# Second norm and residual of the attention stage taken two token tiles late instead of one

## The chip, the cores and the metric

The kernel runs on the 8 cores of one Trainium2 chip. All cores run the same program, each on its own 2048 tokens; they exchange nothing. The time is the device time of the slowest core in microseconds (us). Engines are named as the profile does: PE is TensorE, DVE is VectorE, ACT is ScalarE, POOL is GpSimd, SP is the engine that only issues DMAs.

## What is computed

The input x is 16384 tokens of 1024 numbers (f32). LN stands for the plain layer norm without weights.

```python
# attention over the 16 heads of ONE token (not over the sequence)
qkv = (LN(x) @ W_qkv + b_qkv).reshape(B, S, 16, 192)       # q, k, v of 64 each
scores = einsum('bshd,bsgd->bshg', q, k) / 8
context = einsum('bshg,bsgd->bshd', softmax(scores), v)
x = x + LN(context @ W_out + b_out)
# 8 dense experts, summed
h = LN(x)
acc = sum over e of (silu(h @ Wg[e]) * (h @ Wu[e])) @ Wd[e]
x = x + LN(acc)
```

## The kernel before

One program has three stages: attention (to about 1464 us), experts (64 groups of 512 hidden columns, matmuls almost without a gap, to about 6830 us) and a last norm. The change is in the attention stage alone.

**Tiling.** The 2048 tokens are 16 tiles of 128, one token per partition. Tile t passes through seven steps, S1 to S7, each a Python function that appends instructions to one list per engine. Every engine runs its own list strictly in the order in which it was written; the engines meet only at semaphores. The order in which the loop calls S1 to S7 is therefore the whole schedule.

- S1(t), DVE with ACT: layer norm of x. `ln_stats` (L142 to L160) is three passes over 1024 columns on DVE (L144, L145, L147), a few one-column operations, then Ln and Exp on ACT (L155, L157) and a last DVE operation (L159). DVE then writes `ln1` (L231).
- S2(t), PE with ACT: eight transposes of `ln1` (L207); ACT copies them out to `ln1T` (L210). All three transposing steps (S2, S5, S7) share L207 and L210 and the two halves of `ps_tr`.
- S3(t), PE with ACT: six groups of one bias matmul (L256) and eight matmuls (L260), which alternate between the two halves of `ps_mm`; ACT copies each group out to `qkv` (L265). The third group needs the first one copied out, and so on.
- S4(t), DVE: a copy of v (`vtc`, L275), scores, softmax (its Exp is on ACT, L308), and the weighted sum into `ctxt` (L340). It begins with a wait for the last copy of S3(t).
- S5(t), PE with ACT: eight transposes of `ctxt`, a copy to `ctxT` (L210), then two groups of one bias matmul (L361) and eight matmuls (L364) into `ps_att`, which has two halves, by the parity of t. It waits until S6(t-2) has read the same half (`tok_lna`).
- S6(t), DVE with ACT: `ln_stats_psum` on `ps_att`: a sum on DVE (L164), a Square on ACT (L166) into `scr`, a sum of that on DVE (L168), one-column operations, Ln and Exp on ACT (L176, L178), then DVE normalizes (L380) and adds to x (L384).
- S7(t), DVE with ACT and PE: `ln_stats` on the new x, `ln2tok` (L396), eight transposes and a copy to `ln2T` (L210), which the experts read. After every fourth tile, SP stores the group of four tiles of x (L404) and then, for the first two groups, loads a new group into the same buffer (L407).

The loop of before calls, in iteration t: S2(t), S1(t+1), S3(t), S5(t-1), S6(t-1), S7(t-1), S4(t). In ACT's list this makes, in this order: copy of S2(t); Ln and Exp of S1(t+1); six copies of S3(t); copy of S5(t-1); Square, Ln, Exp of S6(t-1); Ln, Exp and copy of S7(t-1); Exp of S4(t).

The expert stage loads its first weights only when all of the attention stage is over: POOL waits for the last counts of PE, DVE and ACT.

Of the kernel before, what the change touches and what calls it, by code (L numbers as in the profile page):

```python
# [27 lines left out]
def build(mode='full', nt_lim=NT):  # L28
# [46 lines left out]
    def op(k, fn, ch=None, n=1):  # L75
        if ch is not None:
            ch.v += n
            em(k, lambda e, fn=fn, h=ch.h, n=n: fn(e).then_inc(h, n))
            return ch.v
        em(k, fn)  # L80
        return None
# [60 lines left out]
    def ln_stats(src_fn, par):  # L142
        st_ = stats[:, par]
        op('v', lambda v: v.tensor_mul(scr[:, par], src_fn(), src_fn()))  # L144
        op('v', lambda v: v.reduce_sum(st_[:, 0:1], src_fn(), axis=AX.X), VV)  # L145
        VV.wt('v')
        op('v', lambda v: v.reduce_sum(st_[:, 1:2], scr[:, par], axis=AX.X))  # L147
        op('v', lambda v: v.tensor_scalar_mul(st_[:, 0:1], st_[:, 0:1], 1.0 / D), VV)
        VV.wt('v')
        op('v', lambda v: v.tensor_scalar_mul(st_[:, 1:2], st_[:, 1:2], 1.0 / D))  # L150
        op('v', lambda v: v.tensor_mul(st_[:, 2:3], st_[:, 0:1], st_[:, 0:1]), VV)
        VV.wt('v')
        op('v', lambda v: v.tensor_sub(st_[:, 2:3], st_[:, 1:2], st_[:, 2:3]), VV)
        VV.wt('s')
        op('s', lambda s: s.activation(st_[:, 3:4], st_[:, 2:3], AF.Ln, bias=consts[:, 0:1], scale=1.0), SS)  # L155
        SS.wt('s')
        op('s', lambda s: s.activation(st_[:, 4:5], st_[:, 3:4], AF.Exp, scale=consts[:, 1:2]), SS)  # L157
        SS.wt('v')
        return op('v', lambda v: v.tensor_scalar(st_[:, 5:6], st_[:, 0:1], st_[:, 4:5], -1.0,  # L159
                                                 ALU.mult, ALU.mult), VV)  # L160

    def ln_stats_psum(src_fn, par):
        st_ = stats[:, par]
        op('v', lambda v: v.reduce_sum(st_[:, 0:1], src_fn(), axis=AX.X), VV)  # L164
        VV.wt('s')
        op('s', lambda s: s.activation(scr[:, par], src_fn(), AF.Square), SS)  # L166
        SS.wt('v')
        op('v', lambda v: v.reduce_sum(st_[:, 1:2], scr[:, par], axis=AX.X))  # L168
        op('v', lambda v: v.tensor_scalar_mul(st_[:, 0:1], st_[:, 0:1], 1.0 / D), VV)
        VV.wt('v')  # L170
        op('v', lambda v: v.tensor_scalar_mul(st_[:, 1:2], st_[:, 1:2], 1.0 / D))
        op('v', lambda v: v.tensor_mul(st_[:, 2:3], st_[:, 0:1], st_[:, 0:1]), VV)
        VV.wt('v')
        op('v', lambda v: v.tensor_sub(st_[:, 2:3], st_[:, 1:2], st_[:, 2:3]), VV)
        VV.wt('s')
        op('s', lambda s: s.activation(st_[:, 3:4], st_[:, 2:3], AF.Ln, bias=consts[:, 0:1], scale=1.0), SS)  # L176
        SS.wt('s')
        op('s', lambda s: s.activation(st_[:, 4:5], st_[:, 3:4], AF.Exp, scale=consts[:, 1:2]), SS)  # L178
        SS.wt('v')
        return op('v', lambda v: v.tensor_scalar(st_[:, 5:6], st_[:, 0:1], st_[:, 4:5], -1.0,  # L180
                                                 ALU.mult, ALU.mult), VV)
# [18 lines left out]
    def transpose_batch(src_fn, dst):  # L200
        c = n_trb[0]; n_trb[0] += 1
        s_ = c % 2
        if c - 2 in tok_tr_evac:
            QE.wt('t', tok_tr_evac[c - 2])
        tr_tok = None
        for k in range(8):
            tr_tok = op('t', lambda t, k=k, s_=s_: t.transpose(ps_tr[:, s_, k], src_fn(k), ident[:]),  # L207
                        TB if k == 7 else None)
        TB.wt('s', tr_tok)
        ev = op('s', lambda s, s_=s_, dst=dst: s.activation(dst, ps_tr[:, s_], AF.Copy), QE)  # L210
        tok_tr_evac[c] = ev
        return tr_tok, ev
# [4 lines left out]
    def S1(t_i):  # L217
        j, i = divmod(t_i, 4)
        jp = j % 2
        p2 = t_i % 2  # L220
        xt = xf[:, jp, i]
        if t_i == 0:
            GI.wt('v'); VV.wt('v')
        if i == 0:
            XJ = XLa if j % 2 == 0 else XLb
            XJ.wt('v', 16 * (j // 2 + 1))
        ln_stats(lambda xt=xt: xt, p2)
        VV.wt('v')
        if t_i >= 2:
            TB.wt('v', tok_ln1_tr[t_i - 2])  # L230
        tok_ln1_w[t_i] = op('v', lambda v, xt=xt, p2=p2: v.tensor_scalar(  # L231
            ln1[:, p2], xt, stats[:, p2, 4:5], stats[:, p2, 5:6], ALU.mult, ALU.add), VE)

    def S2(t_i):
        p2 = t_i % 2
        VE.wt('t', tok_ln1_w[t_i])
        if t_i == 0:
            GI.wt('t')
        if t_i >= 2:
            MM.wt('v', tok_qkv_mm[t_i - 2])  # L240
        trt, ev1 = transpose_batch(lambda k, p2=p2: ln1[:, p2, k * 128:(k + 1) * 128], ln1T[:, p2])
        tok_ln1_tr[t_i] = trt
        tok_ln1T_ev[t_i] = ev1
# [103 lines left out]
    def S5(t_i):  # L347
        p2 = t_i % 2
        VV.wt('t', tok_hm_done[t_i])
        if t_i >= 2:  # L350
            MM.wt('v', tok_wout_mm[t_i - 2])
        trt2, ev2 = transpose_batch(lambda k, p2=p2: ctxt[:, p2, k * 128:(k + 1) * 128], ctxT[:, p2])
        tok_ctx_tr[t_i] = trt2
        QE.wt('t', ev2)
        if t_i == 0:
            WIo.wt('t')
        if t_i >= 2:
            LNA.wt('t', tok_lna[t_i - 2])
        mt = None
        for n in range(2):  # L360
            op('t', lambda t, n=n, p2=p2: t.matmul(ps_att[:, p2, n], ones1[:],  # L361
                                                   bo_sb[:, n * 512:(n + 1) * 512], start=True, stop=False))
            for k in range(8):
                mt = op('t', lambda t, n=n, k=k, p2=p2: t.matmul(  # L364
                    ps_att[:, p2, n], ctxT[:, p2, k], wout_sb[:, k, n * 512:(n + 1) * 512],
                    start=False, stop=(k == 7)), MM if k == 7 else None)
        tok_wout_mm[t_i] = mt

    def S6(t_i):
        j, i = divmod(t_i, 4)  # L370
        jp = j % 2
        p2 = t_i % 2
        xt = xf[:, jp, i]
        mt = tok_wout_mm[t_i]
        MM.wt('v', mt)
        MM.wt('s', mt)
        psa = lambda p2=p2: ps_att[:, p2].rearrange("p a b -> p (a b)")
        ln_stats_psum(psa, p2)
        VV.wt('v')
        op('v', lambda v, p2=p2, psa=psa: v.tensor_scalar(  # L380
            tmpl[:], psa(), stats[:, p2, 4:5], stats[:, p2, 5:6], ALU.mult, ALU.add), LNA)
        tok_lna[t_i] = LNA.v
        LNA.wt('v', tok_lna[t_i])
        op('v', lambda v, xt=xt: v.tensor_add(xt, xt, tmpl[:]), VV)  # L384
        VV.wt('v')

    def S7(t_i):
        j, i = divmod(t_i, 4)
        jp = j % 2
        p2 = t_i % 2  # L390
        xt = xf[:, jp, i]
        ln_stats(lambda xt=xt: xt, p2)
        VV.wt('v')
        if t_i >= 2:
            QE.wt('v', tok_ln2_ev[t_i - 2])
        w_ln2 = op('v', lambda v, xt=xt, p2=p2: v.tensor_scalar(  # L396
            ln2tok[:, p2], xt, stats[:, p2, 4:5], stats[:, p2, 5:6], ALU.mult, ALU.add), VE)
        VE.wt('t', w_ln2)
        _, ev = transpose_batch(lambda k, p2=p2: ln2tok[:, p2, k * 128:(k + 1) * 128],
                                ln2T[:, :, t_i * 128:(t_i + 1) * 128])  # L400
        tok_ln2_ev[t_i] = ev
        if i == 3:
            QE.wt('y', ev)
            op('y', lambda e, jp=jp, j=j: e.dma_start(xsp_r[:, j], xf[:, jp]), SP, 16)  # L404
            if j + 2 < NJ:
                SP.wt('y')
                op('y', lambda e, j=j, jp=jp: e.dma_start(xf[:, jp], x_r[:, j + 2]),  # L407
                   XLa if (j + 2) % 2 == 0 else XLb, 16)

    S1(0)  # L410
    for t_i in range(nt_lim):
        S2(t_i)
        if t_i + 1 < nt_lim:
            S1(t_i + 1)
        S3(t_i)
        if t_i >= 1:
            S5(t_i - 1)
            S6(t_i - 1)
            S7(t_i - 1)
        S4(t_i)  # L420
    S5(nt_lim - 1)
    S6(nt_lim - 1)
    S7(nt_lim - 1)

# [277 lines left out]
```

How the kernel before makes its waits and increments, by code:

```python
        def wt(self, k, tok=None):  # L71
            t_ = self.v if tok is None else tok
            em(k, lambda e, h=self.h, t=t_: e.wait_ge(h, t))
# [1 line left out]
    def op(k, fn, ch=None, n=1):  # L75
        if ch is not None:
            ch.v += n
            em(k, lambda e, fn=fn, h=ch.h, n=n: fn(e).then_inc(h, n))
            return ch.v
        em(k, fn)
        return None
```

## Time and profile before

| | us |
|---|---|
| runs shown of before | 6951.82 and 7245.42, median 7098.62 |
| the profiled execution | 6951.28 |
| its span, first to last instruction, slowest core | 6949.7 |
| spans of the eight cores | 6936.9 to 6949.7 |
| mean granted TensorE clock (1.0 is 2.4 GHz) | 0.911 on seven cores, 0.912 on one |

The profile records each instruction with its start, its duration and, where its engine had been idle, for how long and which engine's semaphore ended the idle time ("[17.27 <-PE ps_att L364]"). Busy time of an engine that waits for nothing is not what limits a stage; the chain of waits has to be followed from one engine to the next. PE's matmuls overlap, so that eight matmuls in a row show one common duration.

### The profile page before, as it was taken

Reading aid. Unit: us, or ns where it says so; the run is one execution under the profiler, and the core shown is the slowest. Engines: PE = TensorE matmul, PEld = TensorE weight load, DVE = VectorE, ACT = ScalarE, POOL = GpSimd, SP = SyncE. Lnnn points to the kernel's source line nnn. Section 1 sums busy time; section 2 is a strip of 40 time slices with the busy share of each in tenths; the row PEclk is TensorE's granted clock in tenths of the full one; section 3 lists DMA queues with packets and bytes.
Section 4 is the critical chain, followed back from the end, with each engine's and each line's share of the span. In section 5 each row is a group of like instructions: output and inputs, shape, how many; then the busy total and the mean of one; then the engine's idle time right before and its main releaser. Section 6 shows DMA issues by size and latency. Waiting matters only on the chain.

```text
span 6949.7 us, 71337 instructions; the slowest of 8 cores (6936.9 to 6949.7 us)
## 1 busy us (share of the span) xinstructions
PE 5718.3 (82%) x26240; PEld 2567.3 (37%) x26240; DVE 3208.7 (46%) x4436; ACT 792.4 (11%) x1347; POOL 164.9 (2%) x202
## 2 busy tenths in 40 slices
PE   2222222249999999999999999999999999999992
PEld 0111011114444444444444444444444444444441
DVE  4666666743434434334343343443433434334347
ACT  0111111101111111111111111111111111111111
POOL 0000000000000000000000000000000000000000
PEclk7666666669999999999999999999999999999996
DMA  3000000022222222222222222222222222222212
GB/s 73 0 24 0 24 0 12 0 49 37 37 37 37 38 46 45 37 37 37 37 37 37 37 37 43 47 39 37 37 37 37 37 37 37 39 47 43 37 19 97
DMA packets 173421, 247.85 MB, mean 36 GB/s; under 512 B 3616, under 2 KB 134688, under 8 KB 171552
## 3 DMA queue, kind: packets, MB, share of 16 engines
q0 software_dynamic: 169056, 209.74, 18.4%
q1 hardware_dynamic: 4032, 33.56, 1.3%
q8 instruction: 223, 3.65, 0.2%
q14 instruction: 110, 0.90, 0.0%
HBM read 436.22 MB, written 16.78 MB: 65 GB/s over the span
## 4 chain that ended last, share of the span: by engine, by line
PE 80%; DVE 14%; issue 3%; ACT 1%; DMA 1%; another core or an unknown queue 0%; DVEq 0%; ACTq 0%; POOL 0%; POOLq 0%
PE ps_g L508 25%; PE ps_u L513 25%; PE ps_d L539 25%; DVE prod L332 2%; DVE prod L290 2%; PE ps_mm L260 2%; DVE prod L328 2%; DVE prod L286 2%; PE ps_att L364 1%; DVE stats L147 1%; DVE scr L144 1%; DVE stats L145 1%; DMA wd_b<-wd 0%; PE ps_mm L256 0%
## 5 line engine op out<-in xcount | busy, mean ns | idle before, releaser
L523 DVE TENSOR_TENSOR hbuf<-silb,ps_u 128x512 bf16<-128x512 bf16 x1024 | 703.7, 687 | 2888.9 <-PE ps_u L513 2888.9
L508 PE MATMUL ps_g<-ln2T,wg_b 128*128 128x512 bf16 x8192 | 1936.9, 379 | 34.5 <-DMA wd_b<-wd 34.5
L513 PE MATMUL ps_u<-ln2T,wu_b 128*128 128x512 bf16 x8192 | 1936.4, 379 | 0.0
L539 PE MATMUL ps_d<-hbuf,wd_b 128*128 128x512 bf16 x8192 | 1809.7, 379 | 0.0
L549 DVE TENSOR_TENSOR acc<-ps_d,acc 128x512 f32<-128x512 f32 x2016 | 1393.0, 692 | 331.1 <-PE ps_d L539 303.7
L508 PEld LDWEIGHTS ps_g<-ln2T,wg_b 128*128 128x128 bf16 x8192 | 802.0, 98 | 1001.9 <-issue 36.4
L513 PEld LDWEIGHTS ps_u<-ln2T,wu_b 128*128 128x128 bf16 x8192 | 801.8, 98 | 967.9 <-issue 2.2
L539 PEld LDWEIGHTS ps_d<-hbuf,wd_b 128*128 128x128 bf16 x8192 | 801.6, 98 | 966.5
L519 ACT ACTIVATE silb<-ps_g 128x512 bf16<-128x512 f32 x1024 | 612.3, 598 | 4675.3 <-PE ps_g L508 4675.3
L256 PE MATMUL ps_mm<-bq_sb,ones 1*128 1x512 bf16 x96 | 49.0, 510 | 723.0 <-ACT ln1T L210 371.0
L256 PEld LDWEIGHTS ps_mm<-bq_sb,ones 1*128 1x128 bf16 x96 | 9.2, 96 | 773.1 <-issue 773.1
L260 PE MATMUL ps_mm<-wqkv_sb,ln1T 128*128 128x512 bf16 x768 | 245.2, 477 | 0.0
L207 PE MATMUL ps_tr<-ident,ln2tok 128*128 128x128 bf16 x128 | 16.2, 307 | 242.3 <-DVE ln2tok L396 242.3
L480 POOL DMA_DIRECT2D wg_b<-wg x64 | 57.0, 890 | 6491.5 <-PE ps_d L539 5030.1
L332 DVE TENSOR_TENSOR prod<-prod 128x2048 bf16<-128x2048 bf16 (+2 forms) x192 | 162.4, 846 | 20.0
L290 DVE TENSOR_TENSOR prod<-prod 128x2048 bf16<-128x2048 bf16 (+2 forms) x192 | 149.9, 781 | 20.7 <-DVE prod L290 1.0
L328 DVE TENSOR_TENSOR prod<-probsn,vtc 128x4096 bf16<-128x4096 bf16 x64 | 146.3, 2285 | 3.7 <-DVE probsn L314 3.7
L286 DVE TENSOR_TENSOR prod<-qkv 128x4096 bf16<-128x4096 bf16 x64 | 146.0, 2281 | 0.0
L164 DVE TENSOR_REDUCE stats<-ps_att 128x1 f32<-128x1024 f32 x16 | 19.6, 1224 | 259.6 <-PE ps_att L364 259.6
L260 PEld LDWEIGHTS ps_mm<-wqkv_sb,ln1T 128*128 128x128 bf16 x768 | 80.4, 115 | 139.8 <-issue 100.6
L207 PEld LDWEIGHTS ps_tr<-ident,ln2tok 128*128 128x128 bf16 x128 | 12.4, 138 | 249.7 <-issue 249.7
L616 PE MATMUL ps_c<-ident,acc_bf 128*128 128x128 bf16 x128 | 14.8, 290 | 101.0 <-DVE acctok L620 99.9
(80 smaller groups left out, 976.4 us busy)
## 6 DMA issues: line engine op xcount, KB each, us to landing
wg_b<-wg POOLq DMA_DIRECT2D x64, 1024.0 KB, 9.5
wu_b<-wu POOLq DMA_DIRECT2D x64, 1024.0 KB, 13.7
wd_b<-wd POOLq DMA_DIRECT2D x64, 1024.0 KB, 17.8
xf<-x SPq DMA_DIRECT2D x4, 2048.0 KB, 10.6
xspill<-xf SPq DMA_DIRECT2D x4, 2048.0 KB, 7.0
xrel<-xspill SPq DMA_DIRECT2D x4, 2048.0 KB, 8.1
out<-outb SPq DMA_DIRECT2D x16, 512.0 KB, 2.6
wqkv_sb<-wqkv POOLq DMA_DIRECT2D x1, 6144.0 KB, 52.5
```

Source lines behind the costliest of these rows:

```text
L144: op('v', lambda v: v.tensor_mul(scr[:, par], src_fn(), src_fn()))
L260: mt = op('t', lambda t, n=n, b=b, k=k, p2=p2: t.matmul(ps_mm[:, b], ln1T[:, p2, k], wqkv_sb[:, k, n * 512:(n + 1) * 512], start=False, st ...
L286: op('v', lambda v, sl=sl, qap=qap, kap=kap: v.tensor_tensor(prod[:, sl].rearrange("p (h g d) -> p h g d", h=4, g=16), qap, kap, ALU.mult) ...
L290: op('v', lambda v, sl=sl, half=half: v.tensor_add(bass.AP(prod, sl * 4096, [[8192, 128], [1024, 4], [64, 16], [1, half]]), bass.AP(prod, ...
L328: op('v', lambda v, sl=sl, pap=pap, vap=vap: v.tensor_tensor(prod[:, sl].rearrange("p (h d g) -> p h d g", h=4, d=64), pap, vap, ALU.mult) ...
L332: op('v', lambda v, sl=sl, half=half: v.tensor_add(bass.AP(prod, sl * 4096, [[8192, 128], [1024, 4], [16, 64], [1, half]]), bass.AP(prod, ...
L508: gt = op('t', lambda t, par=par, kh=kh, kd=kd, bk=bk, toks=toks: t.matmul(ps_g[:, bk], wg_b[:, par, kd, kh * 128:(kh + 1) * 128], ln2T[:, ...
L513: ut = op('t', lambda t, par=par, kh=kh, kd=kd, bk=bk, toks=toks: t.matmul(ps_u[:, bk], wu_b[:, par, kd, kh * 128:(kh + 1) * 128], ln2T[:, ...
L519: silu_tok[c] = op('s', lambda s, bk=bk, c=c: s.activation(silb[:, c % 2], ps_g[:, bk], AF.Silu), SIL)
L523: mul_tok[c] = op('v', lambda v, kh=kh, bk=bk, c=c, q=q: v.tensor_tensor(hbuf[:, q % 2, kh], silb[:, c % 2], ps_u[:, bk], ALU.mult), MUL)
L539: dt_ = op('t', lambda t, par=par, m=m, mi=mi, kh=kh, q=q: t.matmul(ps_d[:, mi], wd_b[:, par, kh, m * 128:(m + 1) * 128], hbuf[:, q % 2, k ...
L549: tok = op('v', lambda v, m=m, mi=mi, toks=toks: v.tensor_add(acc[:, m, toks], ps_d[:, mi], acc[:, m, toks]), ACC)
```

## The change

S6 and S7 are called for tile t-2 instead of t-1 in iteration t, from iteration 2 on. S5 stays at t-1. Behind the loop, S6(14) and S7(14) follow S5(15), and then come S6(15) and S7(15). No instruction is added or removed; all sizes and buffers stay.

```diff
         S3(t_i)
         if t_i >= 1:
             S5(t_i - 1)
-            S6(t_i - 1)
-            S7(t_i - 1)
+        if t_i >= 2:
+            S6(t_i - 2)
+            S7(t_i - 2)
         S4(t_i)
     S5(nt_lim - 1)
+    if nt_lim >= 2:
+        S6(nt_lim - 2)
+        S7(nt_lim - 2)
     S6(nt_lim - 1)
     S7(nt_lim - 1)
```

## Rows read from the trace of the kernel before

**Rows 1.** Head of the profile's page.
```profile
span 6949.7 us, 71337 instructions; the slowest of 8 cores (6936.9 to 6949.7 us)
```

**Rows 2.** Stretches: length, busy us (instructions) by engine, granted clock, DMA share, GB/s.
```profile
134.00:1464.00 1330.00, 366.75 (x1428) 139.73 (x1427) 919.53 (x1110) 141.16 (x253) 0.00 (x0) 0.62 0.02 8
...
2000.00:4000.00 2000.00, 2000.00 (x9269) 906.70 (x9267) 799.23 (x1159) 230.82 (x386) 60.46 (x72) 1.00 0.23 39
```

**Rows 3.** Waits of 0 to 1400 us: total, times, longest.
```profile
DVE stats L164 <- PE ps_att L364: 249.9, 15, 17.5
...
ACT scr L166 <- DVE stats L164: 93.5, 15, 8.7
```

**Rows 4.** Timeline of iteration 8: start, duration, engine, line, operation [idle before].
```profile
723.32 2.05 PE L260 MATMUL ps_mm<-wqkv_sb,ln1T 128*128 128x512 bf16 x8
...
747.33 1.06 ACT L265 ACTIVATE qkv<-ps_mm 128x512 bf16<-128x512 f32 x2
...
760.27 1.02 ACT L210 ACTIVATE ctxT<-ps_tr 128x1024 bf16<-128x1024 bf16 x1
...
763.99 1.90 PE L364 MATMUL ps_att<-wout_sb,ctxT 128*128 128x512 bf16 x8
766.00 1.23 DVE L164 TENSOR_REDUCE stats<-ps_att 128x1 f32<-128x1024 f32 x1 [17.27 <-PE ps_att L364]
767.32 1.02 ACT L166 ACTIVATE scr<-ps_att 128x1024 f32<-128x1024 f32 x1 [6.03 <-DVE stats L164]
768.44 1.22 DVE L168 TENSOR_REDUCE stats<-scr 128x1 f32<-128x1024 f32 x1 [1.22 <-ACT scr L166]
...
779.89 0.81 DVE L396 TENSOR_SCALAR ln2tok<-xf,stats 128x1024 bf16<-128x1024 f32 x1 [0.18 <-DVE stats L159]
...
782.06 1.02 ACT L210 ACTIVATE ln2T<-ps_tr 128x1024 bf16<-128x1024 bf16 x1 [2.67 <-PE ps_tr L207]
...
854.70 1.22 DVE L164 TENSOR_REDUCE stats<-ps_att 128x1 f32<-128x1024 f32 x1 [17.38 <-PE ps_att L364]
```

**Rows 5.** Timeline of iteration 15, the last, which has no S1.
```profile
1373.61 1.22 DVE L164 TENSOR_REDUCE stats<-ps_att 128x1 f32<-128x1024 f32 x1 [9.80 <-PE ps_att L364]
1374.92 1.02 ACT L166 ACTIVATE scr<-ps_att 128x1024 f32<-128x1024 f32 x1 [8.73 <-DVE stats L164]
```

**Rows 6.** Timeline of iterations 0 (first row) and 1.
```profile
72.15 1.02 DVE L275 COPY vtc<-qkv 128x1024 bf16<-128x1024 bf16 x1 [43.89 <-ACT qkv L265]
...
139.40 0.60 ACT L265 ACTIVATE qkv<-ps_mm 128x512 bf16<-128x512 f32 x1 [1.55 <-PE ps_mm L260]
...
145.62 1.23 DVE L164 TENSOR_REDUCE stats<-ps_att 128x1 f32<-128x1024 f32 x1 [16.44 <-PE ps_att L364]
146.94 1.02 ACT L166 ACTIVATE scr<-ps_att 128x1024 f32<-128x1024 f32 x1 [6.03 <-DVE stats L164]
...
160.17 1.02 DVE L275 COPY vtc<-qkv 128x1024 bf16<-128x1024 bf16 x1
```

**Rows 7.** Timeline behind the loop: S5(15), S6(15), S7(15).
```profile
1440.29 1.02 ACT L210 ACTIVATE ctxT<-ps_tr 128x1024 bf16<-128x1024 bf16 x1 [26.16 <-PE ps_tr L207]
...
1448.70 1.23 DVE L164 TENSOR_REDUCE stats<-ps_att 128x1 f32<-128x1024 f32 x1 [9.77 <-PE ps_att L364]
...
1451.43 1.22 DVE L168 TENSOR_REDUCE stats<-scr 128x1 f32<-128x1024 f32 x1 [1.51 <-ACT scr L166]
...
1462.88 0.81 DVE L396 TENSOR_SCALAR ln2tok<-xf,stats 128x1024 bf16<-128x1024 f32 x1 [0.18 <-DVE stats L159]
```

**Rows 8.** Timeline, PE alone: third and fourth S3 group of iteration 1, fourth of iteration 14.
```profile
129.01 3.60 PE L260 MATMUL ps_mm<-wqkv_sb,ln1T 128*128 128x512 bf16 x8
...
133.08 1.92 PE L260 MATMUL ps_mm<-wqkv_sb,ln1T 128*128 128x512 bf16 x8
...
1285.06 2.77 PE L260 MATMUL ps_mm<-wqkv_sb,ln1T 128*128 128x512 bf16 x8
```

**Rows 9.** DMA issues of 0 to 1600 us: count, KB each, median us to landing.
```profile
xf<-x SPq DMA_DIRECT2D x4, 2048.0 KB, 10.6
```

## The prediction

> **What bounds the kernel now.** I read the page's head first [rows 1], then the stretches [rows 2]. They show two different kernels. From 134 to 1464 us, DVE is busy 919.5 of 1330 us (69%) and PE 366.8 (28%); from 2000 to 4000 us PE is busy all the time, at a granted clock of 1.00. The change only touches the first, so its whole effect must come from what DVE waits for there. The table of waits gives the price of the thing that the change is about [rows 3]: DVE sat idle 249.9 us, 15 times, in front of the first operation of S6 (L164) until the S5 matmuls were done, and once more 9.77 us behind the loop [rows 7], 259.7 us in all. The same table has a second row that matters more: ACT sat idle 93.5 us before the Square of S6 (L166).
>
> The timeline of iteration 8 [rows 4] shows why these differ. DVE is free at 766.00 - 17.27 = 748.73. But ACT starts the first two S3 copies only at 747.33, right behind Ln and Exp of S1(9), and the third and later groups of S3 can't run before that. So the stretch from 748.7 to 766.0 is, in this order: four S3 groups on PE with their copies on ACT, the ctxT copy (760.27 to 761.29), 18 matmuls of S5 (to 765.9), then L164. DVE, ACT and PE form one chain; DVE's next work is S6 and behind it S4.
>
> **What the change does, iteration 2 to 14.** L164 of tile t-2 reads matmuls that were done in the iteration before, so it starts at about 748.73 and is over 1.3 us later. The Square that follows is on ACT, and ACT's list still has the S3 copies and the ctxT copy ahead of it, for S5(t-1) is still called before S6(t-2). It can start at 761.29 and not at 767.32. L168 waits for it, and all else on DVE is behind L168. So what goes is ACT's idle time before the Square: 6.03 us here, made of the S5 matmuls and of L164. The stall of 17.27 is not removed: about 11 us of it stay and stand before L168 instead of L164. For 13 iterations: 93.5 less iteration 1 (6.03, [rows 6]) less iteration 15 (8.73, [rows 5]) = **78.7 us gained**, 6.06 each.
>
> These rows carry the choice between 6 and 17 us. The second S3 group was done at 725.4 (723.32 + 2.05, [rows 4]), the first before it, and ACT had nothing else to do, yet their two copies stood until 747.33 behind the two small operations of S1. A list that is run in order has this effect, and the Square meets it too. The Trainium skill has a rule that read alone speaks for the larger number: "A matmul on TensorE doesn't block a copy on VectorE unless you put a semaphore between them" (Trainium Architecture — The Big Picture, section What this means for kernel authors). By it, DVE would be freed entirely and the sum would be that of the first rival below; by the row, a third engine that both share in order keeps them tied.
>
> **Iteration 15** has no S1, so its S3 copies are early, and the Square waits for the ctxT copy alone. DVE is free at 1373.61 - 9.80 = 1363.81, so that L164 is over before the copy ends at 1374.92 - 8.73 = 1366.19. ACT's idle 8.73 us go: **8.7 gained**.
>
> **Iteration 1** now has no S6 and S7. S4(1) begins when the last S3 copy is done, 139.40 + 0.60 = 140.00, plus 0.1 as in iteration 0 (copy done 72.05, L275 at 72.15): at 140.1 instead of 160.17 [rows 6], **20.1 gained**. Some 14 us of that is only work put off, and comes back behind the loop. The S5(0) matmuls now run under S4(1) and end at about 145.5, with nothing behind them but transposes whose copy is queued after the Exp of S4(1).
>
> **Behind the loop.** Let E = 1448.70 - 9.77 = 1438.93 be the end of S4(15) in before. There ln2tok of tile 15 starts at E + 23.95 [rows 7]. Afterwards S6(14) and S7(14) stand between. Square(14) can start when the ctxT copy ends, E + 2.38; L168 follows 1.12 later (767.32 to 768.44 in [rows 4]); from L168 to ln2tok it is 11.45, and the next operation can start 0.73 behind that: L164(15) at E + 15.7. The S5(15) matmuls are over by then (E + 9.7). Square(15) must let the copy of ln2T(14) go first, which ends 3.19 after ln2tok(14) starts (779.89 to 783.08): E + 18.1. Then 1.12 and 11.45 again: ln2tok(15) at E + 30.7. **6.8 lost.**
>
> **Sum.** 78.7 + 8.7 + 20.1 - 6.8 = 100.7 us. Against the profiled execution of 6951.28 us that gives **6850 us**, 1.4% less. Its span is 6949.7, so 1.6 us lie outside and stay. Of the two runs shown, one (6951.82) is this same time; the median of the two, 7098.62, is pulled up by the other, 4.2% longer, and the same program made both.
>
> **What I cost at nothing.** The copy of ln2T, the transposes of S7 and S2 and their ACT copies lie under the first half of S4 (over 20 us) and move about 6 us earlier with DVE. Without that cover they would cost what rows 4 show from ln2tok to the copy's end, 3.2 us an iteration, about 45 in all. The added wait stands on ACT: nothing but S6's own Ln, then S7's and the Exp of S4(t), is queued behind the Square, and DVE isn't there yet. The store and reload of x move one iteration later. The reload is issued in iteration 5 (9) and first read at the start of iteration 7 (11), so a whole iteration, 88.7 - 6.1 = 82.6 us [rows 4], lies between; a load of this size landed 10.6 us after its issue [rows 9]. Only one seven times as slow would be seen. `ps_att` is given back by S6(t-3) in the iteration before S5(t-1) needs it, so PE gets no new wait. While the Square reads one half of `ps_att`, PE writes the other; no row of before shows just that pair, but the S3 copies run beside matmuls into the other half of `ps_mm`, 0.60 us each [rows 6], and in the worst case I let the Square take double: 1.02 x 14 = 14 us. Below, nothing is excluded but a shorter Square, worth nothing by any row.
>
> **The clock in the attention stage.** Its granted clock is 0.62 [rows 2]: PE goes back and forth between the lower level (1.2 GHz) and the upper (2.4 GHz). Eight matmuls behind a long wait took 3.60 us, and the next eight 1.92 in one iteration and 2.77 in another, so the rise comes somewhere within them [rows 8]. These groups are on the chain. The new spacing can move the rise: if it always came as early as in iteration 1, 0.85 x 13 = 11 us more are gained; if it always came only after the last S3 group, group 4 costs 0.8 more and groups 5 and 6 1.9 each, their bias matmuls with them: 4.6 x 14 = 64 us lost. The work before each rise stays the same, four groups after the same long wait, so I take nothing.
>
> **The rivals.**
> - *The whole stall goes.* 259.7 less what iteration 1 must still wait for its S3 copies (129.18 to 140.1, 10.9) is 248.8: 6702 us, 3.6% faster. For it: the stall is put down to PE alone and the tile's matmuls are long done. Against it: the order of ACT's list, above. It would need ACT to take the Square ahead of the copies. 4 in 100.
> - *The wait is moved, nothing more.* Were the Square or a later step still tied to the S5(t-1) matmuls, iterations 2 to 15 gain nothing and only 20.1 - 6.8 = 13.3 remain: 6938 us. All groups share one counter for matmuls, MM; but the value that S6(t-2) waits for was reached an iteration earlier. A late rise of the clock throughout (100.7 - 64) lands near it, 6915. 7 in 100 for both.
> - *Slower: the expert stage loses its clock.* The stage is some 5300 us of matmuls, so that each 1% of clock is 53 us; from 1.9% on the gain is gone. At 3% less it costs 160 us: 7010 us. The attention stage becomes denser just ahead, and the same program also made a run 294 us longer. Against it: the profiled clock is 1.00, and the expert stage itself is not changed, nor how it is entered. 4 in 100.
>
> **How the numbers follow.** My forecast has 85 in 100, with its own range of 6825 (clock rises early, and 0.2% between cores [rows 1]) to 6885 (double Square, part of a late rise): 6850 is its middle of weight. The wider range is 6820 to 7000: it takes in the moved wait and most of the slower case, and also the middle of two runs, should one of them be 4.2% longer as in before (6850 and 6850 + 294 have 6997 between them). Two per cent is about what a measurement of this kernel can tell from no change; that is 139 us, more than my sum and less than the first rival's. Faster by over 2%: the first rival and a little for a sum of gains that I have too low, 0.06. Slower by over 2% (above 7090): only part of the last case, 0.03. Within: 0.91.
>
> **What the changed profile would show.** DVE's idle time before L164 near zero in iterations 2 to 15, and a new one of 11 to 12 us before L168, put down to ACT L166; hardly any ACT idle time before L166; L364 matmuls beside L166 and L168; an iteration of about 82.6 us; L275 of tile 1 at about 140; the expert stage beginning 100 us earlier. If L168 doesn't wait, the first rival is right. If an iteration stays near 88, the second is, or the clock: then S3's groups 4 to 6 take over 2.8 us. I would be wrong as well if DVE passes or the Square became longer through the new overlap.

## The result, and the profile after

The profiled execution of the changed kernel took 6840.48 us, against 6951.28 before: 110.8 us less. The ratio to the kernel before is 0.984, with a 95% interval of 0.982 to 0.9859: 1.6% faster, within the 2% that count as no change here. The median over all 11 timed runs of the changed kernel is 7686.2 us (before: 7246.72 over 10), because in 8 of the 11, and in 6 of the 10, the cores of one die or of both had a lower mean granted clock and the run took 4% to 17% longer; the ratio above and the results of the experiments below are of runs and cores without this (the three of the changed kernel took 6840.83, 6841.96 and 6842.30 us).

The head of the page after, and two stretches with the columns of [rows 2]:

```profile
span 6838.9 us, 71337 instructions; the slowest of 8 cores (6835.4 to 6838.9 us)
```

```profile
134.00:1363.00 1229.00, 349.74 (x1428) 136.23 (x1426) 918.16 (x1110) 139.84 (x253) 5.06 (x6) 0.64 0.03 11
2000.00:4000.00 2000.00, 2000.00 (x9268) 906.73 (x9267) 800.78 (x1162) 229.87 (x385) 60.48 (x72) 1.00 0.28 39
```

DVE's busy time in the attention stage is what it was in [rows 2] (918.2 against 919.5 us). The first stretch ends at 1363 us 101 us before that of [rows 2], where the forecast put the end of the stage; its last DVE operation in fact starts at 1351.05 us, 112 us earlier than in before (1462.88). The expert stage has the same granted clock of 1.00, and its matmuls again fill the whole stretch. All of the gain is idle time of DVE.

The table of waits (0 to 1400 us; total, times, longest) and the groups of L164 and of the Square (line, engine, operation, count, busy, mean ns, idle before) show where the idle time is now:

```profile
DVE stats L168 <- ACT scr L166: 158.7, 16, 11.9
```

```profile
L164 DVE TENSOR_REDUCE stats<-ps_att 128x1 f32<-128x1024 f32 x16 | 19.5, 1217 | 0.0
...
L166 ACT ACTIVATE scr<-ps_att 128x1024 f32<-128x1024 f32 x16 | 16.4, 1028 | 0.0
```

The row for L164 of [rows 3], 249.9 us, has no successor: L164 never waits. In its place L168 waits 158.7 us for the Square. ACT's idle time before the Square, 93.5 us in [rows 3], is 0.0. The timeline of iteration 9 shows it in order:

```profile
767.38 1.06 ACT L265 ACTIVATE qkv<-ps_mm 128x512 bf16<-128x512 f32 x2
...
768.69 1.22 DVE L164 TENSOR_REDUCE stats<-ps_att 128x1 f32<-128x1024 f32 x1
...
779.11 0.60 ACT L265 ACTIVATE qkv<-ps_mm 128x512 bf16<-128x512 f32 x1 [1.55 <-PE ps_mm L260]
779.61 1.02 ACT L210 ACTIVATE ctxT<-ps_tr 128x1024 bf16<-128x1024 bf16 x1
780.51 1.03 ACT L166 ACTIVATE scr<-ps_att 128x1024 f32<-128x1024 f32 x1
...
781.21 1.90 PE L364 MATMUL ps_att<-wout_sb,ctxT 128*128 128x512 bf16 x8
781.64 1.22 DVE L168 TENSOR_REDUCE stats<-scr 128x1 f32<-128x1024 f32 x1 [11.73 <-ACT scr L166]
...
783.36 1.90 PE L364 MATMUL ps_att<-wout_sb,ctxT 128*128 128x512 bf16 x8
...
793.09 0.81 DVE L396 TENSOR_SCALAR ln2tok<-xf,stats 128x1024 bf16<-128x1024 f32 x1 [0.18 <-DVE stats L159]
```

L164 starts at once behind S1(10). The Square starts as the ctxT copy ends, 11.8 us after L164 did, with the S3 copies from 767.38 to 779.71 ahead of it. The matmuls of S5 (L364) now run beside the Square and beside L168, off the chain.

The start of S4 in iterations 1 and 14, and the steps behind the loop:

```profile
138.36 1.03 DVE L275 COPY vtc<-qkv 128x1024 bf16<-128x1024 bf16 x1 [10.87 <-ACT qkv L265]
...
1203.47 1.03 DVE L275 COPY vtc<-qkv 128x1024 bf16<-128x1024 bf16 x1
...
1320.45 1.22 DVE L164 TENSOR_REDUCE stats<-ps_att 128x1 f32<-128x1024 f32 x1
...
1336.11 1.22 DVE L164 TENSOR_REDUCE stats<-ps_att 128x1 f32<-128x1024 f32 x1
...
1338.48 1.02 ACT L166 ACTIVATE scr<-ps_att 128x1024 f32<-128x1024 f32 x1
...
1351.05 0.81 DVE L396 TENSOR_SCALAR ln2tok<-xf,stats 128x1024 bf16<-128x1024 f32 x1 [0.18 <-DVE stats L159]
```

In before, L275 of iteration 14 started at:

```profile
1313.07 1.02 DVE L275 COPY vtc<-qkv 128x1024 bf16<-128x1024 bf16 x1
```

With [rows 6] and these, and the starts of L275 in iteration 15 (1388.22 us before, 1269.81 after), the stage can be cut into the parts of the forecast, each as the distance between two starts, before less after:

| part | forecast | measured |
|---|---|---|
| iteration 1, L275 to L275 (88.02 to 67.89) | 20.1 | 20.1 |
| iterations 2 to 14 (1152.90 to 1065.11) | 78.7 | 87.8 |
| iteration 15 (75.15 to 66.34) | 8.7 | 8.8 |
| behind the loop, end of S4(15) to ln2tok(15) (23.95 to 30.60) | -6.8 | -6.7 |
| all | 100.7 | 110.1 |

(S4(15) itself took 0.07 us less.) The load of the first weights, before all this, ended 1.7 us earlier than in before, and from ln2tok(15) on the kernel took 1.0 us more; with these two it is the 110.8 us of the spans. One part is off by 9.1 us, the thirteen middle iterations: 6.75 us each instead of 6.06.

### The profile page after: what moved, and what is told of

It is laid out like the page before. It is cut to its first block, busy times and chain, and to the rows that moved or that the text cites. A ratio compares the mean times of both kernels' runs of the same rounds, so it can differ in the third digit from the quotient of the medians.

```text
span 6838.9 us, 71337 instructions; the slowest of 8 cores (6835.4 to 6838.9 us)
## 1 busy us (share of the span) xinstructions
PE 5703.1 (83%) x26240; PEld 2563.7 (37%) x26240; DVE 3206.6 (47%) x4436; ACT 789.7 (12%) x1347; POOL 165.0 (2%) x202
## 4 chain that ended last, share of the span: by engine, by line
PE 80%; DVE 14%; issue 3%; ACT 1%; DMA 1%; another core or an unknown queue 0%; DVEq 0%; ACTq 0%; POOL 0%; POOLq 0%
PE ps_g L512 26%; PE ps_u L517 26%; PE ps_d L543 26%; DVE prod L332 2%; DVE prod L290 2%; DVE prod L328 2%; DVE prod L286 2%; PE ps_mm L260 2%; DVE stats L147 1%; DVE scr L144 1%; DVE stats L145 1%; DMA wd_b<-wd 0%; PE ps_mm L256 0%; DVEq L73 0%
## 5 line engine op out<-in xcount | busy, mean ns | idle before, releaser
L168 DVE TENSOR_REDUCE stats<-scr 128x1 f32<-128x1024 f32 x16 | 19.5, 1220 | 158.7 <-ACT scr L166 158.7
L265 ACT ACTIVATE qkv<-ps_mm 128x512 bf16<-128x512 f32 x96 | 55.5, 593 | 177.1 <-PE ps_mm L260 177.1
```

## The experiments

The theory T: ACT runs its list in order, and the list decides. S3's copies are held up by Ln and Exp of S1(t+1), which wait for the DVE passes of S1(t+1), and DVE comes to those only behind S4(t-1); everything behind them on the list, the Square included, is late with them. The rivals: R1, the remaining 11.7 us belong to the S6 work itself or to what is shared while it runs; R2, the distance between S5 and S6 in tiles is what counts. A last question is where the 9.1 us came from.

**Distance two, and S1 called behind S3.** Edit to the changed kernel:

```diff
-        if t_i + 1 < nt_lim:
-            S1(t_i + 1)
         S3(t_i)
+        if t_i + 1 < nt_lim:
+            S1(t_i + 1)
```

> The changed kernel, with the call of S1(t+1) moved behind S3(t), so that Ln and Exp of S1(t+1) stand behind the six S3(t) copies on ACT's list. Theory of the order of ACT's list: S3(t) then runs under the second half of S4(t-1), the Square meets a free ACT, DVE's wait before L168 falls from 11.7 us to about 1.2, an iteration from 81.9 to 71.4 us; iteration 1 no longer waits 10.9 us before L275. Total 6840 - 13 x 10.5 - 10.9 + 1.5 = about 6694 us. Rival, that the rest of the stall comes from the S6 work itself or from PE and PSUM being shared: the wait stays near 11 us and the time near 6840.

Measured: 6695.66, 6696.50 and 6698.59 us; ratio to the kernel before 0.9574, interval 0.9432 to 0.9716 (6696.50 to 6951.28 alone is 0.963). From the waits of 134 to 1250 us and the timeline:

```profile
DVE stats L168 <- ACT scr L166: 22.6, 16, 2.3
```

```profile
742.59 0.60 ACT L265 ACTIVATE qkv<-ps_mm 128x512 bf16<-128x512 f32 x1 [1.55 <-PE ps_mm L260]
...
756.58 1.00 ACT L210 ACTIVATE ctxT<-ps_tr 128x1024 bf16<-128x1024 bf16 x1
...
757.90 1.22 DVE L164 TENSOR_REDUCE stats<-ps_att 128x1 f32<-128x1024 f32 x1
...
759.21 1.02 ACT L166 ACTIVATE scr<-ps_att 128x1024 f32<-128x1024 f32 x1 [1.63 <-DVE stats L164]
760.33 1.22 DVE L168 TENSOR_REDUCE stats<-scr 128x1 f32<-128x1024 f32 x1 [1.22 <-ACT scr L166]
```

The last S3 copy is done 8 us before S1 begins on DVE (S4 ends at 751.6), and ACT waits for L164 instead of the other way round. An iteration takes 71.5 us. R1 falls: the same S6, on the same engines, beside the same S5 matmuls, waits 1.2 us. This version beats both kernels, by 145 us the changed one.

**Distance one, and S1 called behind S3.** The same edit to the kernel before.

> The kernel before (S6, S7 one tile late), with the call of S1(t+1) moved behind S3(t). Theory of the order of ACT's list: the stall before L164 was mostly S3 held up by S1's Ln and Exp; now only the S5 chain is left in it (ctxT copy about 5 us after S4 ends, 18 matmuls of about 7.1 us behind a long wait), so L164 waits about 7 us instead of 17.2. Total 6951 - 14 x 10 + 1.5 = about 6811 us: more than the change under study gives, without it. Rival, that only the distance of S6 from S5 matters: the stall stays at 17 us and the time at 6951.

Measured: 6810.84 and 6811.93 us. L164 now waits only for what S5 needs:

```profile
764.57 1.22 DVE L164 TENSOR_REDUCE stats<-ps_att 128x1 f32<-128x1024 f32 x1 [7.12 <-PE ps_att L364]
```

R2 falls too: with the order of calls changed and not the distance, the kernel gains more (140 us) than with the distance changed alone (111 us). Of the 17.3 us of stall, 10 were the place of S1 on ACT's list. The last two versions also price the change when S1 stands behind S3: 6811 - 6696 = 115 us.

**Distance one, S5 ahead of S1.** Edit to the kernel before: the calls in the order S3(t), S5(t-1), S1(t+1), S6(t-1), S7(t-1).

```diff
-        if t_i + 1 < nt_lim:
-            S1(t_i + 1)
         S3(t_i)
         if t_i >= 1:
             S5(t_i - 1)
+        if t_i + 1 < nt_lim:
+            S1(t_i + 1)
+        if t_i >= 1:
             S6(t_i - 1)
```

> The kernel before (S6, S7 one tile late) with the calls in the order S3(t), S5(t-1), S1(t+1), S6(t-1), S7(t-1): the ctxT copy stands ahead of Ln and Exp of S1 on ACT. Theory of the order of ACT's list: the S5 chain then starts right when S4(t-1) ends and runs beside S1(t+1): transposes and copy 2.4 us, 18 matmuls about 7.4 us, so that L164 can start 9.8 us after S4, when DVE comes from S1 after 6.7 us: a wait of about 3 us in place of 7.1 with S1 ahead, 14 x 4.0 less than 6811, about 6755 us. The change under study would then still be worth about 60 us on top (the run with both gave 6696). Rival, that one tile of distance can't be hidden: 6811 us as before.

Measured: 6764.05 us, 9 more than expected. The S5 matmuls still start on a PE at its lower level (the first eight took 3.6 us), and the wait is 3.5 us, not 3:

```profile
809.48 1.22 DVE L164 TENSOR_REDUCE stats<-ps_att 128x1 f32<-128x1024 f32 x1 [3.51 <-PE ps_att L364]
```

A mere swap of calls at distance one is thus worth 187 us. The version with distance two and S1 behind S3 is 68 us faster still, with S1 ahead of S5 instead of behind it; the two together in one order were not run.

**The Square taken off ACT.** Edit to the changed kernel, in `ln_stats_psum`:

```diff
-        VV.wt('s')
-        op('s', lambda s: s.activation(scr[:, par], src_fn(), AF.Square), SS)
-        SS.wt('v')
+        VV.wt('v')
+        op("v", lambda v: v.tensor_copy(tmpl[:], src_fn()), VV)
+        VV.wt("v")
+        op("v", lambda v: v.tensor_mul(scr[:, par], tmpl[:], tmpl[:]), VV)
+        VV.wt('v')
```

> The changed kernel, with the Square of S6 taken off ACT: DVE copies ps_att to tmpl and squares it there into scr (two DVE passes more, 1.2 to 1.3 us each). Theory of the order of ACT's list: it is not the Square that is slow, its place on the list is; DVE now runs through L174 and waits before L180 instead, for the Ln and Exp that stand behind the same S3 and ctxT copies. They start near where the Square started, 3 us earlier than now: 13 x 2.9 less about 1 us for the three S6 that gain nothing, total about 6803 us, wait before L180 8 to 9 us. Rival, that the Square is what ties DVE down: the 11.7 us go but for the two passes added, total about 6720.

Measured: 6798.09 us. The lines of `ln_stats_psum` move down by two from here, so Ln is L178 and L180 of the changed kernel is L182:

```profile
758.37 0.29 ACT L178 ACTIVATE stats<-stats,consts 128x1 f32<-128x1 f32 x1
...
759.16 0.21 DVE L182 TENSOR_SCALAR stats<-stats 128x1 f32<-128x1 f32 x1 [6.44 <-ACT stats L180]
```

The wait moved to the next thing that S6 needs of ACT, and Ln starts where the Square had started, right behind the ctxT copy. What is gained (42 us) is that 3.1 us of the chain (from the Square's start to Ln's, 780.51 to 783.61 in the changed kernel) now pass during the wait. The wait is 6.4 us, not the 8 to 9 that I had written: I had left out the two added passes, 2.6 us, which fill it; the total holds them and was right within 5 us. The expectation's rival, that the Square itself ties DVE down (6720 us), did not come.

**S6 and S7 called before S5, behind S3.** Edit to the changed kernel:

```diff
         S3(t_i)
-        if t_i >= 1:
-            S5(t_i - 1)
         if t_i >= 2:
             S6(t_i - 2)
             S7(t_i - 2)
+        if t_i >= 1:
+            S5(t_i - 1)
         S4(t_i)
```

> The changed kernel, with S6(t-2) and S7(t-2) called behind S3(t) but before S5(t-1): the ctxT copy now stands behind S6 and S7 on ACT's list, the S5 matmuls behind the S7 transposes on PE's. Theory of the order of ACT's list: the Square moves up by what stood between it and the last S3 copy, the ctxT copy, 0.8 us; the wait before L168 falls from 11.7 to about 10.9 us; total 6840 - 13 x 0.8 - 1 = about 6829 us. Rival, that the S5 work is what ties the Square: most of the 11.7 us go, total under 6750 us.

Measured, cores 0 to 3: spans of 6824.4 to 6830.0 us, expected about 6829. Core 0:

```profile
776.35 0.60 ACT L265 ACTIVATE qkv<-ps_mm 128x512 bf16<-128x512 f32 x1 [1.55 <-PE ps_mm L260]
776.85 1.02 ACT L166 ACTIVATE scr<-ps_att 128x1024 f32<-128x1024 f32 x1
777.97 1.22 DVE L168 TENSOR_REDUCE stats<-scr 128x1 f32<-128x1024 f32 x1 [11.58 <-ACT scr L166]
```

With the whole of S5 out of its way, the Square gained the ctxT copy and nothing more: the remaining stall is S3's. (Here the wait is 11.58 and not 10.9 because the fourth S3 group of this iteration took 2.81 us; over the thirteen iterations L275 to L275 is 81.3 us, against 81.9.)

**S6 and S7 called before S3.** Edit to the changed kernel:

```diff
-        S3(t_i)
-        if t_i >= 1:
-            S5(t_i - 1)
         if t_i >= 2:
             S6(t_i - 2)
             S7(t_i - 2)
+        S3(t_i)
+        if t_i >= 1:
+            S5(t_i - 1)
         S4(t_i)
```

> The changed kernel, with S6(t-2) and S7(t-2) called before S3(t), so that the Square and all that follows it stand ahead of the six S3 copies on ACT. Theory: the wait before L168 falls to 2.3 us or less (as behind the loop), but the S3 copies start only behind the ln2T copy, so that DVE waits for them before L275, about 15 us: vtc is reached some 5.4 us later in each iteration, 14 x 5.4, total about 6915 us. Rival, that the Square's place on the list is all that matters: 10 us less per iteration, about 6700.

Measured: 6946.12 us; the direction was right, the size wrong by 31 us. The timeline:

```profile
733.32 1.22 DVE L168 TENSOR_REDUCE stats<-scr 128x1 f32<-128x1024 f32 x1 [1.22 <-ACT scr L166]
...
745.84 1.01 PE L207 MATMUL ps_tr<-ident,ln2tok 128*128 128x128 bf16 x8 [66.06 <-DVE ln2tok L396]
...
747.32 3.59 PE L260 MATMUL ps_mm<-wqkv_sb,ln1T 128*128 128x512 bf16 x8
...
762.70 1.04 DVE L275 COPY vtc<-qkv 128x1024 bf16<-128x1024 bf16 x1 [17.11 <-ACT qkv L265]
```

The Square meets a free ACT (L168 waits 1.2 us), and DVE waits 17 us before L275 instead. My expectation counted only ACT's list. PE has one too: the transposes of S7(t-2) stand ahead of S3 on it, PE was idle 66 us in front of them, and so all six S3 groups start late, not four. An iteration takes 88.8 us, as before the change.

**Padding: where the 9.1 us came from.** The fourth S3 group of an iteration is the one in which the clock of PE rises: in iteration 14 of before the granted clock was 0.50 during the third group (3.60 us), 0.67 during the fourth (2.77) and 1.00 during the fifth (1.90). In iterations 2 to 14 the fourth took 2.48 to 2.85 us before (34.7 in all), and 1.90 to 2.20 us after (26.0 in all): 8.7 us of the 9.1. The groups ahead of it behind the same wait are the same. Iteration 14 after, against 2.77 us in [rows 8]:

```profile
1182.39 1.98 PE L260 MATMUL ps_mm<-wqkv_sb,ln1T 128*128 128x512 bf16 x8
```
 Two runs put idle DVE operations between S7(t-2) and S4(t) of the changed kernel, to make an iteration, and PE's pauses in it, longer without touching the lists of PE and ACT:

```diff
             S7(t_i - 2)
+            for _ in range(5):          # 2 in the other run
+                VV.wt('v')
+                op('v', lambda v: v.tensor_mul(tmpl[:], scr[:, 0], scr[:, 0]), VV)
         S4(t_i)
```

> The changed kernel with five idle DVE operations (128x1024 products of scr into tmpl, 1.33 us each with their wait) between S7(t-2) and S4(t), so that nothing changes but the length of an iteration: 81.9 + 6.65 = 88.6 us, the length it had before. Question: the fourth S3 group of an iteration took 2.67 us on average before and 2.00 after, which gave 0.6 us per iteration more than forecast. Theory A, that the place of the clock's rise follows the length of the iteration: the group comes back to 2.4 to 2.8 us, the iteration to about 89.2, total about 6840 + 14 x 6.65 + 13 x 0.6 = 6941 us. Theory B, that what the change moved on PE (S5 matmuls beside the Square, transposes 6 us nearer behind them) set it: the group stays at 2.0 us, total about 6933 us.

> The same with two such operations: iteration 81.9 + 2.7 = 84.6 us. Theory A: a fourth S3 group somewhere between 1.9 and 2.8 us, another mean than at 81.9 and at 88.6, with each length its own; total 6877 us plus at most 10. Theory B: 2.0 us as in the changed kernel, total about 6877 us.

Measured: 6937.31 us with five and 6883.65 us with two. Iteration 14 with five:

```profile
1265.02 2.33 PE L260 MATMUL ps_mm<-wqkv_sb,ln1T 128*128 128x512 bf16 x8
```

PE's groups of S3 over the attention stage (count, busy us, mean ns), in the changed kernel, with five and with two operations:

```profile
L260 PE MATMUL ps_mm<-wqkv_sb,ln1T 128*128 128x512 bf16 x768 | 233.8, 459 | 0.0
```

```profile
L260 PE MATMUL ps_mm<-wqkv_sb,ln1T 128*128 128x512 bf16 x768 | 238.6, 466 | 0.0
```

```profile
L260 PE MATMUL ps_mm<-wqkv_sb,ln1T 128*128 128x512 bf16 x768 | 241.7, 472 | 0.0
```

The same 768 matmuls in the same order take 5 to 8 us more, with idle DVE operations as the only change; in before it was 245.2 us (477 ns). With five operations (6.45 us an iteration, measured) an iteration takes 88.7 us, and the fourth group 1.94 to 2.53 us, 2.32 on average: half of the way back to before's 2.67. With two it takes 1.90 to 2.79, seven of thirteen over 2.6. All eight cores show this: the mean of the fourth group over iterations 2 to 14 is 1.96 to 2.00 us on the cores of the changed kernel, 2.42 to 2.47 with two operations and 2.28 to 2.33 with five; before, it is 2.63 to 2.67 on seven cores and 2.46 on core 7. So theory A holds in kind: the length of the iteration moves the rise of the clock, and not in one direction (84.8 us is worse than 81.9 and than 88.7). It doesn't hold in size: at before's own length the group isn't as slow as before's. Nor is the length all that counts: with S6 and S7 called before S5 an iteration is 81.3 us long, nearly that of the changed kernel, and the group took 1.90 to 2.82 us (core 0). What makes up the other half is open. Neither theory's total decides it, since 6937 lies between 6941 and 6933.

## Why the prediction was right, and where it wasn't

- *The bound, and what the change does.* Right. DVE, ACT and PE were one chain, and ACT's idle time before the Square, not DVE's before L164, was the price of the change. The stall of 17.3 us became one of 11.7 before L168, as the forecast said ("about 11 us of it stay"). The run with S5 moved away confirms what is left in it, the run with S1 moved confirms why.
- *The first rival, beside which the prediction named a rule.* The whole stall of an iteration going gave 6702 us, and the measured 6840 shows the tie that stood against it: an engine in between, ACT, that runs its list in order. With S1 moved behind S3 the tie is gone and 6696 us come out, near the rival's number; an iteration is then 17.2 us shorter than before (88.7 to 71.5). The rule, in the Trainium skill (Trainium Architecture — The Big Picture, section What this means for kernel authors), is that a matmul holds up a copy on VectorE only through a semaphore. The trace agrees with the rule as it is worded: in the changed kernel L168 waited 11.73 us for the Square on ACT and for no matmul.
- *Iterations 1 and 15, and behind the loop.* Right within 0.1 us each.
- *Costed at nothing.* Right. The Square took 1028 ns, against 1024 before; the doubling that I allowed for (14 us) did not come. In the changed kernel only about the last 0.6 us of a Square lie beside the S5 matmuls (from 780.91 us, in iteration 9); with S1 behind S3 all of it does in the iteration shown (759.21 to 760.23, matmuls from 758.34 on), and it took 1022 ns on average over the 16. The reload of x stayed without a trace in DVE's waits.
- *Iterations 2 to 14.* The mechanism was right and the size too small: 87.8 us instead of 78.7. The term that failed is the clock in the attention stage, which I took as nothing with "the work before each rise stays the same". It does stay the same, and the rise still moved, by 0.67 us of the fourth group in each iteration; I had its bound right (up to 11 us gained). Another 0.1 us an iteration is that the Square, without a wait of its own, starts 0.12 us before the ctxT copy ends (780.51 against 780.63); the two make some 10 us, one more than was measured, and that one is not traced.
- *The range. This is the step that failed.* My own range for the forecast, 6825 to 6885, holds the profiled 6840 us. The wide one, 6820 to 7000, does not hold the median over all runs, 7686 us. I had set its top by "the middle of two runs, should one of them be 4.2% longer as in before": one run's excess as the size, and one run in two as the most. In its place the runs showed 8 of 11 longer, by 4% to 17%. Two runs of before could show that such runs exist, but neither how frequent nor how long they are.
- *The rival of a lost clock.* I priced it as 3% of the expert stage's clock, 160 us, and as an effect of the change. In the profiled execution the stage kept its 1.00. The one longer run with a trace (S6 and S7 called before S5, cores 6 and 7) shows the loss in that very stage: the granted clock was 1.00 from 2000 to 6000 us and 0.81 from 6100 to 6700 us, and these two cores ended 127 us behind cores 0 to 3. The kernel before had such runs too, up to 8108.65 us, so nothing here ties them to the change; what brings them on is open.
- *The other rivals.* The whole stall didn't go, and the moved wait did not come: iterations 2 to 15 gained 96.6 us, not nothing.

## What to carry to other kernels

Before work is set further apart, write down each engine's list in order and find the first item that is not ready; the gain ends there, whatever the semaphore in the profile's row is put down to. Here two one-column operations of the next tile's norm stood ahead of six copies, and moving one call behind them gave 140 us, where taking S6 and S7 one tile later gave 111, and both together 255. An "idle before" row of an engine that is 11% busy can be the best price of a change: ask for the idle time of the engine that comes second on the chain, too.

## What the runs showed of the hardware that I had not expected

The place where PE's clock rises from 1.2 to 2.4 GHz within a burst of matmuls moved with the length of the loop around it, with the same matmuls behind the same wait: the group in question took 1.90 to 2.20 us at an iteration of 81.9 us, mostly 2.6 to 2.8 at 84.8, 1.94 to 2.53 at 88.7, and 2.48 to 2.85 at 88.7 in the kernel before. The length alone doesn't fix it, as the last two show. It is much the same on all eight cores, so it is no scatter, but no row of the kernel before says which value a new length will give. It is worth up to 0.9 us an iteration here, and a change of a few us per iteration can gain or lose it.
